# Order of the end: the first pass's expert layers, outputs and first adds moved ahead of other work

## The reference

```python
# per step, x is (8, 64, 128, 128)
x = x + conv(_ln_c(x))            # norm over channels; conv: group norm, w1, relu, w2, plus its input
t = tokens(x)                     # (8, 16384, 64)
t = t + _L0_ffn_ref(_ln_t(t), gate_w, gate_b, weight1, weight2)
...
# _L0_ffn_ref, 32 experts, 8 tokens each
logits = einsum('bsd,ed->bse', x, gate_w) + gate_b
vals, idx = top_k(softmax(logits, axis=1).transpose(0, 2, 1), 8)
pooled = einsum('bked,bke->bed', gathered, topv)
h = concatenate([pooled.transpose(1, 0, 2), ones], axis=-1)
h = gelu(einsum('ebd,edh->ebh', h, weight1))
h = concatenate([h, ones], axis=-1)
out = einsum('ebh,eho->ebo', h, weight2)
weighted = einsum('beo,bke->bkeo', out.transpose(1, 0, 2), topv)
outputs = zeros.at[batch, flat_idx].add(weighted)   # 256 token places a batch, some twice
```

## Time and profile before

| | us |
|---|---|
| median of 3 runs | 627.07 |
| lowest, highest | 625.97, 628.53 |
| span of the profiled execution | 630.2 |
| TensorE busy | 541.1 (86%) |
| VectorE busy | 487.1 (77%) |
| ScalarE busy | 436.5 (69%) |
| GpSimd busy | 188.7 (30%) |

### The profile page before, as it was taken

The page is one execution under the profiler, slowest core; times in us unless marked ns, Lnnn a source line. Parts: engine busy times, 40 slices in busy tenths (PEclk is TensorE's granted clock), DMA queues, the critical chain, the costliest instruction groups (busy, mean ns, idle before and its releaser), DMA issues.

```text
span 630.2 us, 14170 instructions
## 1 busy us (share of the span) xinstructions
PE 541.1 (86%) x5732; PEld 274.7 (44%) x5732; DVE 487.1 (77%) x950; ACT 436.5 (69%) x651; POOL 188.7 (30%) x116
## 2 busy tenths in 40 slices
PE   3659999998989898998999899989898988977982
PEld 1333444444444444444444444434443433344762
DVE  5575565789888978897899779987888798799520
ACT  2455788787977796779767976897687855974110
POOL 1008362115302440235022602080308044130045
PEclk9956998999999989998999799989998999976595
DMA  8960245623661457144714453435411265520000
GB/s 193 196 152 14 101 129 158 170 80 91 189 179 62 109 156 190 57 136 134 200 70 135 133 157 113 136 101 167 134 43 61 91 182 152 160 81 5 6 16 19
DMA packets 26752, 73.38 MB, mean 116 GB/s; under 512 B 4152, under 2 KB 4152, under 8 KB 22592
## 3 DMA queue, kind: packets, MB, share of 16 engines
q1 hardware_dynamic: 25664, 71.44, 41.2%
q0 software_dynamic: 1024, 1.05, 0.6%
HBM read 38.40 MB, written 34.08 MB: 115 GB/s over the span
## 4 chain that ended last, share of the span: by engine, by line
PE 44%; DVE 28%; ACT 12%; issue 11%; DMA 2%; another core or an unknown queue 1%; POOL 0%; SPq 0%; ACTq 0%; DVEq 0%; POOLq 0%
PE st L372 10%; PE cv L383 8%; PE bc L494 6%; PE tl L400 6%; PE cv L391 5%; DVE us L949 5%; ACT junk L810 5%; DVE xs L959 5%; DVE lg L947 3%; PE tl L409 3%; DVE cnd L1041 2%; DVE top_i L1046 2%; ACT tok L775 2%; DVE us L951 2%; DMA xs<-in_x 2%
## 5 line engine op out<-in xcount | busy, mean ns | idle before, releaser
L1437 POOL TENSOR_TENSOR xs<-xs,us 128x1024 f32<-128x1024 f32 x64 | 150.7, 2376 | 360.3 <-DVE xs L959 177.4
L959 DVE SCALAR_TENSOR_TENSOR xs<-cv,vecs,xs 128x1024 f32<-128x1024 f32 x64 | 82.0, 1282 | 25.2 <-PE cv L391 24.9
L770 ACT ACTIVATE hid<-cv,b1n 128x1024 f32<-128x1024 f32 x64 | 71.3, 1115 | 39.3 <-PE cv L383 38.8
L803 ACT ACTIVATE sqc<-us 128x1024 f32<-128x1024 f32 x64 | 67.6, 1056 | 42.3 <-DVE us L949 41.6
L400 PEld LDWEIGHTS tl<-ident,xs 128*128 128x128 f32 x512 | 64.4, 196 | 56.9 <-issue 56.9
L951 DVE CUSTOM_DVE_ANT_0 us<-us,bc 128x1024 f32<-128x1024 f32 x60 | 73.0, 1216 | 19.0 <-PE bc L494 17.7
L949 DVE TENSOR_TENSOR us<-xs,bc 128x1024 f32<-128x1024 f32 x60 | 73.0, 1216 | 17.5 <-PE bc L494 17.1
L810 ACT ACTIVATE junk<-us 128x1024 bf16<-128x1024 f32 x64 | 67.5, 1055 | 20.5 <-DVE gsum L951 19.9
L372 PE MATMUL st<-xs,stat_w 128*32 128x256 f32 x1024 | 72.6, 404 | 8.9 <-DMA xs<-in_x 8.9
L400 PE MATMUL tl<-ident,xs 128*128 128x128 f32 x512 | 77.1, 296 | 1.6 <-ACT lg L785 1.6
L409 PE MATMUL tl<-xs,gcen 128*32 128x256 f32 x1024 | 71.7, 400 | 7.4 <-ACT tok L775 7.4
(11 more groups left out here) (210 smaller groups left out, 657.0 us busy)
## 6 DMA issues: line engine op xcount, KB each, us to landing
xs<-in_x SPq DMA_DIRECT2D x64, 512.0 KB, 7.0
out_rows<-tok SPq DMA_DIRECT2D x64, 512.0 KB
us<-in_e_w SPq DMA_DIRECT2D x8, 260.0 KB
xs<-in_e_w SPq DMA_DIRECT2D x8, 256.0 KB
sqc<-out_rows,idx_all POOLq DMA_INDIRECT x16
out_rows<-sqc,idx_all POOLq DMA_INDIRECT x16
vecs<-in_b SPq DMA_DIRECT2D x4, 0.2 KB, 14.0
gate_bias<-in_gate_b SPq DMA_DIRECT2D x4, 0.1 KB, 12.4
```

The lines of the kernel that those rows point to most:

```text
L959: nc.vector.scalar_tensor_tensor(out=xu, in0=cv[:], scalar=vecs[:, 3:4], in1=xu, op0=ALU.add, op1=ALU.add).then_inc(x1_done, 1)
L1437: nc.gpsimd.tensor_tensor(xu, xu, su, ALU.add).then_inc(s_done, 1)
```

## The change

On TensorE the transposes of the first pass (`experts_turn(0)`) move ahead of batch 7's merge matmul. The second layer of the first pass is cut in two halves of 16 experts, one ahead of `fold_last_sums` and one behind it. `expert_rows(0)` and `add_rows(0)` move ahead of the second pass's pooling (`experts_in(1)`) and first layer, and `add_rows(1)` ahead of its transposes. On VectorE `turned(0)` moves ahead of the merge of batch 7, `expert_outs(0)` and `contributions(0)` ahead of the copy of the pooled rows, `token_norm` is cut into `token_variances` and `token_scales` with `contributions(0)` between them, and `result_rows(1)` moves ahead of `last_turned`.

```diff
--- before.py
+++ after.py
@@ -643,16 +643,17 @@
                         mm = pe.transpose(h_banks[i][:, P * k:P * k + P], hg[:, CH * i + P * k:CH * i + P * k + P], ident[:])
                     mm.then_inc(t2_done, 1)
 
-            def experts_down(p):
+            def experts_down(p, e0, e1):
 
                 pe.wait_ge(ht_ready, 4 * p + 4)
-                for e in range(0, NE, 2):
+                for e in range(e0, e1, 2):
                     for k in range(2):
                         for par in range(2):
                             col = 32 * (2 * (e // 4) + k) + NB * ((e + par) % 4)
                             mm = pe.matmul(pd[C * par:C * par + C, NB * (e // 2):NB * (e // 2) + NB], ew2[:, e + par, k, :],
                                            ht[:, col:col + NB], start=(k == 0), stop=(k == 1), skip_group_check=True)
-                mm.then_inc(l2_done, 1)
+                if e1 == NE:
+                    mm.then_inc(l2_done, 1)
 
             def last_experts_down():
 
@@ -711,17 +712,18 @@
             experts_in(0)
             spread_stat(NB, "E", 3)
             experts_up(0)
+            experts_turn(0)
             spread_stat(NB, "M", NB - 1)
-            experts_turn(0)
+            experts_down(0, 0, NE // 2)
             fold_last_sums()
-            experts_down(0)
+            experts_down(0, NE // 2, NE)
+            expert_rows(0)
             spread_pixels(3)
+            add_rows(0)
             experts_in(1)
-            expert_rows(0)
             experts_up(1)
-            add_rows(0)
+            add_rows(1)
             experts_turn(1)
-            add_rows(1)
             last_experts_down()
             add_rows(2)
             last_expert_rows()
@@ -1194,15 +1196,18 @@
                 dve.wait_ge(rcent_done, 1)
                 nc.vector.tensor_tensor(zz, zz, ws.unsqueeze(2).broadcast_to([P, 6 * GATHERS, C]), ALU.mult).then_inc(z_ready, 1)
 
-            def token_norm():
+            b0, b1 = PASSES[1]
+            n0, n1 = GATHERS * b0, GATHERS * b1
+            late_shape = [P, n1 - n0, C]
+            late_zs = zs.rearrange("p b g c -> p (b g) c")[:, n0:n1]
+            late_mean, late_var, late_y, late_a, late_rs, late_ws = (tr[:, i, n0:n1] for i in range(6))
+
+            def token_variances():
 
                 b0, b1 = PASSES[1]
-                n0, n1 = GATHERS * b0, GATHERS * b1
-                shape = [P, n1 - n0, C]
+                shape, zz, mean, var = late_shape, late_zs, late_mean, late_var
                 r = rows_all.rearrange("p b g c -> p (b g) c")[:, n0:n1]
-                zz = zs.rearrange("p b g c -> p (b g) c")[:, n0:n1]
                 q = late[:, CH:CH + (n1 - n0) * C].rearrange("p (n c) -> p n c", c=C)
-                mean, var, y, a, rs, ws = (tr[:, i, n0:n1] for i in range(6))
                 dve.wait_ge(rows_in[3], 16 * GATHERS * (b1 - b0))
                 lns(nc.vector.tensor_reduce(mean, r, AX.X, ALU.add))
                 lns(nc.vector.tensor_scalar(mean, mean, 1.0 / C, None, ALU.mult))
@@ -1210,6 +1215,11 @@
                 lns(nc.vector.tensor_tensor(q, zz, zz, ALU.mult))
                 lns(nc.vector.tensor_reduce(var, q, AX.X, ALU.add))
                 nc.vector.tensor_scalar(var, var, 1.0 / C, EPS, ALU.mult, ALU.add).then_inc(rvar_ready, 1)
+
+            def token_scales():
+
+                b0, b1 = PASSES[1]
+                shape, zz, var, y, a, rs, ws = late_shape, late_zs, late_var, late_y, late_a, late_rs, late_ws
                 dve.wait_ge(ry_ready, 2)
                 newton(lns, var, y, a, 0.0)
                 lns(nc.vector.scalar_tensor_tensor(out=rs, in0=a, scalar=1.5, in1=y, op0=ALU.add, op1=ALU.mult))
@@ -1369,9 +1379,9 @@
                 top_places(7, i)
             candidates(7)
             merge_values(NB - 2, link)
+            turned(0)
             use_spread(NB, "M", NB - 1)
             link = merge_pixels(NB, NB - 1)
-            turned(0)
             last_sums()
             lns(nc.vector.tensor_tensor(id2[:], ident[:, 0:C], ident[:, C:P], ALU.add))
             nc.vector.tensor_reduce(mask8[:].rearrange("p (q s) -> p q s", q=2),
@@ -1380,14 +1390,15 @@
             last_sums_folded()
             merge_values(NB - 1, link)
             diagonals(3)
-            token_norm()
             expert_outs(0)
+            token_variances()
+            contributions(0)
+            token_scales()
             pooled(1)
-            contributions(0)
             equal_pixels(3)
             result_rows(0)
+            result_rows(1)
             last_turned()
-            result_rows(1)
             last_expert_outs()
             result_rows(2)
             contributions(1)
```

## The result

The changed kernel takes 622.45 us (median of 6 runs, 620.87 to 623.93) against 627.89 for the kernel before on the same chip (6 runs, 625.97 to 630.4). The ratio is 0.9902, 95% interval 0.9881 to 0.9923: 1% faster.

What follows compares the result with a forecast made beforehand. It took TensorE to bound the end, GpSimd's scatters being the near rival. The 3.9 us won on the second layer went to waits, slow adds and a copy, leaving +1.05 us: 627.07 to 628.1 us, range 624.8 to 631.6.

Steps and rivals of the forecast that it cites:

- Step 8: GpSimd's scatters begin 4.1 us earlier, but the head start ends in idle time of the queue; sum +1.05 us.
- Steps 1 to 3: First pass's end: transposes hidden, second layer over at 586.0 (3.9 us won), outputs from 587.6, broadcast over at 592.4.
- Steps 4 to 7: Second pass on TensorE: add_rows(0) 3.7 us at low clock, pooling 1.0, first layer 6.2, last layer 1.0 us late.
- step 7: TensorE between second pass's first layer and L662: 3.9 us in place of 5.41, so L662 starts at 607.6.
- theory B: From the experiments, not the prediction: TensorE's clock brought the gain; no chance given.
- That TensorE slows beside scatters: Earlier scatters slow add_rows(1) and the transposes on TensorE, +1.8 us each: 4.6 us in all, 631.7; chance 0.17.
- That the scatters hold back the tail: Scatters piled up cause the late waits; spreading them takes away say 3.5 us: 624.6; chance 0.12.
- That the transposes keep the clock high: First pass's transposes fill TensorE's idle time and keep its clock high to the end: -6.7 us, 621.4; chance 0.05.

Runs made afterwards that it cites:

- e7: The kernel before, unchanged, profiled a second time; one run, 66.2 us from the first pass's pooling matmuls to the end of the span.
- e3: The kernel before with one added wait on GpSimd, the first scatter waiting for the second result rows; ratio to before 1.005.
- e9: e5 with the pixel broadcast also moved ahead of expert_rows(0) on TensorE; ratio to the kernel before 0.995.
- e10: The changed kernel without the second scatters of batches 4 to 7, twelve in place of sixteen; ratio to the kernel before 0.984.
- e5: The changed kernel with result_rows(0) ahead of pooled(1) and equal_pixels(3) on VectorE; 622.1 us, ratio to the kernel before 0.989.

## Why the prediction was wrong, by its steps

**The step that failed: 8, with the sentence ahead of the parts that the queue and the last row are late together.** Step 8 took the head start of the scatters, 4.1 us, and lost it in waits for the second, the third and the last rows. It had found the right term: 627.07 - 4.1 = 623.0, within the spread of what was measured, though the term was too small: the first scatter came 6.3 us earlier. The mistake was to take waits of one trace as a cost of the order. The last four steps of VectorE that wait for TensorE, the three in the earlier trace rows from 612.71 on and the one below, stood 2.9 us apart in the profile of before:

```profile
615.57 0.42 DVE L1341 TENSOR_TENSOR us<-tl,tv_all 128x256 f32<-128x256 f32 x1 [2.44 <-remote]
```

In all other profiles these steps are 0.9 to 2.5 us apart; I carried the delay over whole. It was an accident of one execution, since e7 and e3 have the same order on TensorE without it, and even there it cost 0.3 us, since the scatters stood back to back up to the thirteenth. In the changed kernel the last rows are ready at +48.0, and the fourteenth scatter, the first that needs them, starts at +51.8.

**Steps 1 to 3 held.** Second half of the second layer over at +22.1 (forecast 586.0, +22.4), TensorE idle 1.63 (1.6), outputs from +23.7 (587.6, +24.0), broadcast over at +28.4, where the chain goes on (592.4, +28.8). The first half took 2.27 instead of 3.47, with the clock at full for most of it (until +16.1), but nothing waits for it.

**Steps 4 to 7: right terms, wrong clock.** add_rows(0) was forecast at 3.7 and took 2.4 to 2.8 in the four profiles with the early rise, with the clock rising inside; the pooling 0.6 for 1.0; the layer started at +31.8 (forecast +33.9) and took 3.6 (6.2). In e9 and e10, where the clock rose late, the sizes are nearer to the forecast: 3.68 and 3.52 for the adds, 5.5 for the layer, which started at +33.0 in e10. So the low clock was not an error of size but a case; four profiles of the changed TensorE order had the early rise and one the late one. Even in that one the second pass is not late: its last layer (L663, L662 before) starts at +42.6 in e10, at +39.4 in the changed kernel, and was at +42.9 before; step 7 put it at +44.0. What the early rise is worth can be estimated from the pair e10 and changed: first scatter 1.2 us, last rows 2.9 us. Between before (+40.3) and e10 (+35.2), both with a late rise, lie 5.1 us. By these single profiles that is the gain of the order alone, and theory B is the smaller part. The copy of the pooled rows cost 0.35, as forecast (0.4).

**The rivals.** That TensorE slows beside scatters fell: in the changed kernel the last two groups of the layer and the second adds ran beside scatters from 594.81 on at full pace, 1.91 and 2.00 us. That the scatters hold back the tail had nearly the right time, 624.6, by a wrong mechanism: they were the end itself. That the transposes keep the clock high has the nearest time of all, 621.4, and that is luck: its sum needs a clock that stays high to the end, and the head start of the scatters is not in it. It was half seen: the clock was up from +9.3 to +16.1 in place of +8.7 to +12.1, and then fell during the small second-layer matmuls. These runs do not show which of the transposes, the merge and the first half kept it up, and the rule of the Trainium skill (TensorE: Matmul & The Clock Gate, part 4 on PE-mode transpose) that transposes do not count is tested by no run here.

**What stays open** is what makes the clock rise early. With output transposes, broadcast and adds in this order it rose at +29.1 to +30.0 four times and once at +37.0; with the broadcast first, once, at +36.6. But it moves within the order of before too: +36.0 and +35.9, and +33.2 in e3, where it had also been up a second time from +16.1 to +19.5. That the order is the cause is not shown: one order alone spreads over 8 us.

## What to carry to other kernels

Where an engine works through a queue of equal steps to the end, look at when its first step can start, and add up the queue; what feeds its later steps counts only where the queue is seen empty. A queue whose gaps are all its own is the bound, even if its last step starts right behind its producer. A wait that the trace puts down to nothing known should be seen in a second profile before it is carried into a sum.

## What the runs showed of the hardware that was not expected

A scatter of 128 rows costs GpSimd 1.39 us on average: 0.97 of its own, and mostly 0.30 to 0.32 between two, but 0.65 to 0.69 ahead of the third scatter of each group of four. That third is the first of its group that the code makes wait for the landing of an earlier scatter, the one on the same batch two places ahead. The trace names that landing only where the gap is longer (0.82 in the changed kernel, 1.88 in e10) and calls the 0.66 "issue", so for these the landing is my reading of the code. The whole queue was the same to 0.3 us over 16 scatters in nine of eleven profiles, whatever TensorE did; in e5 and e9 the queue waited for rows.

The same 16 adds of 128x64 took 1.9 to 2.0 us at full clock, 3.7 at half, and 2.7 with the rise inside. In the first profile of before, the four last groups of TensorE's work reached VectorE 2.9 us apart. For the last two the clock had a part in it: it fell to 0.50 at 613.3, when TensorE had nothing to do, and their adds took 1.97 and 1.91 us. But the first two were late although the granted clock read 1.00 in 609 to 613: by TensorE's rows their matmuls ended at 610.4 and 612.4, and VectorE went on at 612.7 and 615.6. In e7 such a stretch shows 1.00 as well and no delay:

```profile
605.00:609.00 4.00, 3.95 (x32) 2.93 (x24) 2.15 (x3) 0.00 (x0) 3.04 (x4) 1.00 0.07 25
```

I have no cause for the difference.
